# First round's mix in four banks, with its gates and routing placed between the first adapter's folding and the others'

## The reference, cut to what matters

```python
W = weights[condition]                     # 16 small 64x64 matrices
y = einsum('bct,bcd->bdt', x, W)           # "mix"
result = y @ W_base.T + b_base
probs = softmax(y @ W_gate.T); top 2 of 8 experts, renormalised -> route_w
h = einsum('bnd,erd->bner', y, A) * route_w
x = x + result + einsum('bner,eor->bno', h, B)
# second layer
y = einsum('bsi,boi->bso', x, weight[adapter_ids])     # adapter_ids are 3 to 7
scores = 8 * softmax(y @ Wr.T + br)
x = x + 2 * einsum('bshr,hor,bsh->bso', y @ A.T, B, scores)
```

## Time and profile before

| | |
|---|---|
| median of three runs | 749.4 us (748.09 to 749.75) |
| profiled execution | 748.57 us, span 746.9 us |
| busy, share of the span | PE 724.3 us (97%), DVE 335.3 (45%), ACT 114.1 (15%), POOL 57.8 (8%) |
| granted clock of PE, mean | 0.992 of 2.4 GHz |
| chain that ended last | PE 81%, issue 8%, DVE 4%, DMA 4% |

### The profile page before, as it was taken

How to read it: one execution, slowest core, us unless ns; L and a number is a source line. 1 busy time by engine, 2 the same in 40 slices (tenths; PEclk the granted TensorE clock), 3 DMA queues, 4 the chain that set the end, 5 groups by cost and what they waited for, 6 DMA issues and landing times.

```text
span 746.9 us, 12572 instructions
## 1 busy us (share of the span) xinstructions
PE 724.3 (97%) x4502; PEld 647.4 (87%) x4502; DVE 335.3 (45%) x887; ACT 114.1 (15%) x309; POOL 57.8 (8%) x115
## 2 busy tenths in 40 slices
PE   7999899999999999999999999998999999999996
PEld 7999887898888888888889888787889888998996
DVE  2000196136534644354535563464427552574644
ACT  1222300111111111111111111111111211120111
POOL 1222300001100010001000110000000100010100
PEclk9999999999999999999999999999999999999998
DMA  7999993037721883159504871277415951476552
GB/s 262 340 417 365 392 403 119 1 117 294 250 80 63 295 315 125 56 181 394 195 29 176 314 286 48 86 259 279 173 57 183 405 179 57 168 301 236 208 192 72
DMA packets 38709, 156.31 MB, mean 209 GB/s; under 512 B 8836, under 2 KB 11908, under 8 KB 28420
## 3 DMA queue, kind: packets, MB, share of 16 engines
q1 hardware_dynamic: 27714, 78.72, 28.4%
q0 software_dynamic: 9216, 71.31, 25.9%
q10 hardware_dynamic: 1730, 5.58, 1.9%
HBM read 133.24 MB, written 22.35 MB: 208 GB/s over the span
## 4 chain that ended last, share of the span: by engine, by line
PE 81%; issue 8%; DVE 4%; DMA 4%; POOL 2%; ACT 0%; POOLq 0%; ACTq 0%; DVEq 0%
PE base_ps L333 16%; PE base_ps L334 16%; PE base_ps L335 16%; PE mix_both L353 7%; DMA adapter<-folded 4%; PE low_ps L401 4%; PE out_ps L401 4%; PE mix_both L366 3%; PE base_ps L342 2%; POOL adapter L943 2%; PE out_ps L333 2%; PE out_ps L334 2%; PE out_ps L335 2%; DVE w_lo L683 1%; PE low_ps L366 1%
## 5 line engine op out<-in xcount | busy, mean ns | idle before, releaser
L333 PE MATMUL base_ps<-yT,w_hi 128*128 128x512 f32 (+1 forms) x576 | 214.7, 373 | 1.3 <-DVE xT L803 1.1
L335 PE MATMUL base_ps<-yT,w_hi 128*128 128x512 f32 (+1 forms) x576 | 211.5, 367 | 0.0
L334 PE MATMUL base_ps<-yT,w_lo 128*128 128x512 f32 (+1 forms) x576 | 211.3, 367 | 0.0
L687 DVE TENSOR_TENSOR yT<-mix_both,yT 128x512 fp32r<-128x512 f32 x64 | 44.2, 691 | 240.9 <-ACT yT L560 240.9
L333 PEld LDWEIGHTS base_ps<-yT,w_hi 128*128 128x128 f32 x576 | 108.5, 188 | 20.8 <-DVE xT L803 4.0
L335 PEld LDWEIGHTS base_ps<-yT,w_hi 128*128 128x128 f32 x576 | 108.4, 188 | 18.1
L334 PEld LDWEIGHTS base_ps<-yT,w_lo 128*128 128x128 f32 x576 | 108.6, 189 | 15.4
L342 PE MATMUL base_ps<-ag_raw,stage 128*128 128x136 f32 x640 | 76.0, 283 | 2.2 <-issue 2.2
L342 PEld LDWEIGHTS base_ps<-ag_raw,stage 128*128 128x128 f32 x640 | 75.9, 193 | 2.4 <-issue 2.4
L957 POOL DMA_DIRECT2D adapter<-folded x60 | 31.9, 532 | 576.5 <-PE low_ps L401 503.8
L699 DVE TENSOR_TENSOR x1T<-xT,x1T 128x256 fp32r<-128x256 f32 x120 | 45.3, 420 | 65.1 <-ACT x1T L567 65.1
(11 more groups left out here) (150 smaller groups left out, 747.3 us busy)
## 6 DMA issues: line engine op xcount, KB each, us to landing
adapter<-folded POOLq DMA_DIRECT2D x63, 1088.0 KB, 7.1
stage<-in_w SPq DMA_DIRECT2D x40, 512.0 KB, 8.0
x_rows<-in_x SPq DMA_DIRECT2D x32, 512.0 KB, 6.0
xT<-in_x_turned SPq DMA_DIRECT2D x16, 1024.0 KB, 7.5
out<-xT SPq DMA_DIRECT2D x28, 512.0 KB, 2.7
folded<-adapter ACTq DMA_DIRECT2D x10, 544.0 KB, 6.7
w_raw<-in_w SPq DMA_DIRECT2D x8, 256.0 KB, 8.0
w_raw<-in_w SPq DMA_DIRECT2D x4, 512.0 KB, 12.1
```

Of the source, the lines that this page charges most:

```text
L333: pe.matmul(dst, st_hi, mv_lo, start=start, stop=False, skip_group_check=True)
L334: pe.matmul(dst, st_lo, mv_hi, start=False, stop=False, skip_group_check=True)
L335: return pe.matmul(dst, st_hi, mv_hi, start=False, stop=stop, skip_group_check=True)
L687: dve.tensor_tensor(yT[:, 1, k, :], mix_ps[k % 2][:, :], yT[:, 0, k, :], ALU.subtract).then_inc(yT_lo_done, 1)
```

## The change

- SP loads `x_rows` and `g_raw` of round 0 before the second adapter's units instead of after the last adapter's.
- PE does mix and gates of round 0 after the first adapter's fold, before the loop over the others. ACT, DVE and POOL get their part of that work (both halves of mix, the copies of the gates, the routing with its Exp, and the split of `g_raw`) at the same place in their lists.
- The mix of round 0 goes through four banks instead of two (`mix_bank`); gates wait for each block as they come to it.
- The second copy of a folded unit goes to `lg` instead of `hg`, since `hg` now holds the gates' result during the other folds.

The core of the diff:

```diff
+        def mix_bank(q, r, k):
+            return hg_banks[k % 4] if isinstance(q, int) and r == 0 else mix_ps[k % 2]
...
             load_wc(0, 0)
             total = adapters_in_use(sp)
+            load_x(0, 0)
+            sp.dma_start(g_raw[:, :, 1, :], g0).then_inc(g_landed, 16)
             with sp.Fori(1, total) as n:
...
-            load_x(0, 0)
-            sp.dma_start(g_raw[:, :, 1, :], g0).then_inc(g_landed, 16)
             for k in range(KC):
                 load_w(k, 0)
...
-                if k >= 2:
-                    pe.wait_ge(yT_lo_done, at(q, r, KC, k - 1))
+                banks = 4 if isinstance(q, int) and r == 0 else 2
+                if k >= banks:
+                    pe.wait_ge(yT_lo_done, at(q, r, KC, k - banks + 1))
...
-                        if t == 0 and k in (0, KC - 1):
+                        if t == 0 and isinstance(q, int) and r == 0:
+                            if k == 0 or k >= 5:
+                                pe.wait_ge(yT_lo_done, max(5, k + 1))
+                        elif t == 0 and k in (0, KC - 1):
                             pe.wait_ge(yT_lo_done, at(q, r, KC, KC - 1 if k == 0 else KC))
+                        if t and k == 0 and isinstance(q, int) and r == 0:
+                            pe.wait_ge(yT_lo_done, 5 + t)
...
             fold(0)
+            for k in range(KC):
+                mix(0, 0, k)
+            pe.wait_ge(g_split, 1)
+            gates(0, 0)
             total = adapters_in_use(pe)
             with pe.Fori(1, total) as n:
                 fold(n)
             pe.wait_ge(unit_copied, KC * total + BANKS)
-            for k in range(KC):
-                mix(0, 0, k)
             iteration(0, 0, l1=False)
...
             take_adapter(0, e, False)
+            for k in range(KC):
+                yT_high(0, 0, k)
+            route_exp(0, 0)
             total = adapters_in_use(act)
...
             for k in range(KC):
                 yT_low(0, 0, k)
+            for t in range(TILES):
+                copy_hg(0, 0, t)
+            routing(0, 0)
             for k in range(KC):
                 split(w_hi[:, k, 0:T], w_lo[:, k, 0:T], w_raw[:, k, 0:T], w_landed[k], k)
```

More of the change, by code:

```diff
@@ L349, in mix @@
                     pe.wait_ge(wc_landed, at(q, r, 16 * PER, 16 * PER))
-                if k >= 2:
-                    pe.wait_ge(yT_lo_done, at(q, r, KC, k - 1))
+                banks = 4 if isinstance(q, int) and r == 0 else 2
+                if k >= banks:
+                    pe.wait_ge(yT_lo_done, at(q, r, KC, k - banks + 1))
                 for t in range(TILES):
-                    mm = pe.matmul(mix_ps[k % 2][:, t * P:(t + 1) * P], x_rows[:, t, k * P:(k + 1) * P], wc[:, t, :],
+                    mm = pe.matmul(mix_bank(q, r, k)[:, t * P:(t + 1) * P], x_rows[:, t, k * P:(k + 1) * P], wc[:, t, :],
                                    start=True, stop=True, skip_group_check=True)
@@ L451, in iteration @@
                 first = isinstance(q, int) and r == 0
-                if first:
-                    pe.wait_ge(g_split, 1)
-                gates(q, r)
+                if not first:
+                    gates(q, r)
                 for k in range(KC):
@@ L546, in take_unit @@
                 act.copy(adapter[:, 0, c, 0, :], base_ps[c % BANKS][:, 0:HG])
-                act.copy(hg[:, c % 4, :], base_ps[c % BANKS][:, 0:HG]).then_inc(unit_copied, 1)
+                act.copy(lg[:, c % 4, :], base_ps[c % BANKS][:, 0:HG]).then_inc(unit_copied, 1)
             def take_adapter(n, e, again):
@@ L559, in yT_high @@
                 act.wait_ge(yT_done, at(q, r, KC, k + 1))
-                act.copy(yT[:, 0, k, :], mix_ps[k % 2][:, :]).then_inc(yT_hi_done, 1)
+                act.copy(yT[:, 0, k, :], mix_bank(q, r, k)[:, :]).then_inc(yT_hi_done, 1)
             def x1T_high(q, r, i):
@@ L580, in lwT_high, with route_exp @@
                 act.copy(lwT[:, 0, toks], low_ps[:, toks]).then_inc(lwT_hi_done, 1)
+            def route_exp(q, r):
+                act.wait_ge(route_step, at(q, r, ROUTE_STEPS, 6))
+                act.activation(top_exp[:, :, :], top_d[:, :, :], ACT.Exp).then_inc(top_exp_done, 1)
             def iteration(q, r, l1=True, ahead=True):
@@ L585, in iteration @@
                     x1T_high(q, r - 1, 1)
-                act.wait_ge(route_step, at(q, r, ROUTE_STEPS, 6))
-                act.activation(top_exp[:, :, :], top_d[:, :, :], ACT.Exp).then_inc(top_exp_done, 1)
-                if l1:
+                    route_exp(q, r)
                     for i in range(2, PER):
@@ L609, in _ @@
                 take_adapter(n, e, True)
-            for k in range(KC):
-                yT_high(0, 0, k)
             iteration(0, 0, l1=False)
@@ L686, in yT_low @@
                 dve.wait_ge(yT_hi_done, at(q, r, KC, k + 1))
-                dve.tensor_tensor(yT[:, 1, k, :], mix_ps[k % 2][:, :], yT[:, 0, k, :], ALU.subtract
+                dve.tensor_tensor(yT[:, 1, k, :], mix_bank(q, r, k)[:, :], yT[:, 0, k, :], ALU.subtract
                                   ).then_inc(yT_lo_done, 1)
@@ L844, in iteration @@
             def iteration(q, r, l1=True, ahead=True, toks=ALL):
-                copy_hg(q, r, 0)
                 if l1:
+                    copy_hg(q, r, 0)
                     x1T_low(q, r - 1, 0)
-                copy_hg(q, r, 1)
-                if l1:
+                    copy_hg(q, r, 1)
                     x1T_low(q, r - 1, 1)
[L851 to L854, removed]
+                    copy_hg(q, r, 2)
+                    copy_hg(q, r, 3)
+                    routing(q, r)
                     for i in range(2, PER):
@@ L942, in low_of_adapter @@
                     pool.wait_ge(unit_copied, KC * n + c + 1 + BANKS)
-                    pool.tensor_tensor(adapter[:, 0, c, 1, :], hg[:, c % 4, :], adapter[:, 0, c, 0, :], ALU.subtract
+                    pool.tensor_tensor(adapter[:, 0, c, 1, :], lg[:, c % 4, :], adapter[:, 0, c, 0, :], ALU.subtract
                                        ).then_inc(folded_lo, 1)
             low_of_adapter(0)
+            pool.wait_ge(g_landed, 16)
+            pool.tensor_copy(g_hl[:, :, 0, :], g_raw[:, :, 1, :]).then_inc(g_split_hi, 1)
+            pool.wait_ge(g_split_hi, 1)
+            pool.tensor_tensor(g_hl[:, :, 1, :], g_raw[:, :, 1, :], g_hl[:, :, 0, :], ALU.subtract).then_inc(g_split, 1)
             total = adapters_in_use(pool)
@@ L966, in iteration @@
                         load_adapter(q, r, i)
[L969 to L972, removed]
             for p in range(2):
```

## The result

The changed kernel takes 753.52 us (median of 10 runs, 751.08 to 757.49) against 748.32 for the kernel before (10 runs, 746.48 to 752.07): ratio 1.0071, interval 1.005 to 1.0092. It is 5.2 us slower; I had forecast slower by 2.1. The profiled execution is one of its longer ones, 756.89 us with a span of 755.2, 8.3 more than that of before.

A forecast was written before the change was run, and what follows sets the result against it. PE, busy 97% of the span, bounds the kernel, so only waits and clock count. Minus 2.6, minus 1.3, plus 3.1, plus 1.7, plus 1.2 give plus 2.1 us: 750.7 from 748.57, forecast 751.0, range 746.5 to 753.6.

The forecast's parts named there:

- Direction: Whole kernel: slower by 2.1 us; chance of slower 0.47, same 0.35, faster 0.18.
- Base's start: PE in round 0, after the last fold: base begins at 105.45 us, 2.2 later than before.
- the wait for x_rows: PE, first fold to round 0's mix: x_rows lands at 28.4, PE is done at 25.3; plus 3.1 us.
- Mix in four banks, minus 2.6: Round 0's mix on PE: no waits between block pairs, 7.84 us instead of 10.44; minus 2.6.
- Routing, minus 1.3: PE ahead of the transposes at 121.09: the wait for routing's last step on DVE goes; minus 1.3 us.
- The clock, plus 1.7: Behind PE's wait for x_rows: 3.4 us at half speed, plus 1.7 us (0 to 1.9).
- The loads that now come later, plus 1.2: Ahead of base's second half, round 0: xT lands at 131.0, PE wants the bank at 130.7; plus 1.2 us.
- the store's landing: Last folded-adapter store, issued at 106.1: lands 4.5 us later, between 3.0 alone and 7.0 behind the crowded queue.
- the rest of the chain: SP's loads behind the last store: 20.2 us from round 1's first x issue to the landing of xT.
- `xT` *is really late: Rival, round 0's second half: store takes 7.0 us, PE waits 3.7; 753.2 to 754.0, clock plus 1.7 more; chance 0.14.
- The rule of the Trainium skill: Last store: DMA engines serve queues in turn, so half rate, some 4.7 us, wait 1.4; the sum didn't need it.

The follow-up runs named there:

- the two runs that isolate it: Four-bank mix alone put on the kernel before: 745.89 us, ratio 0.9972; and two-bank mix put back in the best kernel: 748.58 us, ratio 0.9994.
- with the transposes: Changed kernel plus unread transposes, 14 ahead of round 0's mix and 16 ahead of base's second half: 751.16 us, ratio 1.0034 to the kernel before.
- the best kernel: Changed kernel with round 0's wc issued by POOL, x_rows early on SP, and round 1's loads ahead of the stores' wait: 745.82 us, ratio 0.9967.
- `xT` first: Changed kernel with SP loading round 0's xT ahead of round 1's x_rows and wc: 751.99 us, ratio 1.0066 to the kernel before.
- routing late: The best kernel with round 0's gate copies and routing back behind DVE's splits, and its Exp behind ACT's folds: 746.71 us, ratio 0.997.

## Why the prediction was right and wrong

- **Direction: right. Base's start, 105.39 against 105.45: luck.** Terms of opposite sign cancelled: the first fold ended 2.1 us sooner than I took it to, for a reason that has no place in my sum; so the wait for x_rows was 4.43 and not 3.1, though x_rows landed 0.8 earlier; the clock cost 1.4 more than I had, and mix took 0.6 less. With `wc` on POOL this first wait and its clock are worth 4.7 us by the ratios, where I had 3.1 + 1.7 = 4.8. That fit is luck in part: in the traces base begins 6.4 us earlier there (99.01), and the 4.7 is uncertain by some 2.
- **Mix in four banks, minus 2.6: right in kind, undersized in the trace.** 3.2 us by the timelines of mix (10.4 to 7.2: a block takes 0.90 us, where I had 0.93, and nothing is left uncovered ahead of the gates, where I had 0.4), 2.0 to 2.1 in the medians of the two runs that isolate it, of which the second also waits for `xT`.
- **Routing, minus 1.3: not shown in the time.** The wait is gone from the trace and comes back with the edit, 1.97 us long and with a fall of the clock behind it, but its price in the median is not resolved.
- **The clock, plus 1.7: undersized.** In the profiled execution 3.1 us behind the first wait, since the low clock lasted 6.8 us and not the 3.4 that I took from the kernel before. That it falls is not sure either: with the transposes PE still stood idle for 3.65 us and stayed at 2.4 GHz.
- **The loads that now come later, plus 1.2: this step failed.** The mechanism was the right one, down to the issue of the last store at 106.1, but the wait was 4.21 us. Two terms made the difference of 3.0: the store's landing (6.6 against 4.5; the row of before said 7.0, and I took a milder value because I counted 1.2 MB of W_base still to move, when SP's queue moved 1.74 MB in that time, and b1, issued at 99.1, landed at 113.3) and the rest of the chain (21.2 against 20.2). PE wanted the bank at 130.7, as in my sum. And the clock fell behind that wait, another 2.3 us, which my sum did not hold; it stood in the rival with 7.0 us for the store. Taking this wait away wins 4.1 us of the median, against the 1.2 of my sum. The rival `xT` *is really late* is what happened in the trace: a wait of 4.21 us where it had 3.7, and the clock down once more. That its 753.2 to 754.0 hold the measured 753.5 is luck in part, for they are without that fall; with the 1.7 that the rival gives for it they would be 754.9 to 755.7.
- The rule of the Trainium skill, page "DMA: Bandwidth & Descriptors", section "Queues, rings and completion order", by which I estimated some 4.7 us for the store whatever stood on SP's queue, is not borne out as I applied it: 6.6 with loads of W_base and b1 still on it and 2.7 with nothing on it. That the engines take turns is neither shown nor refuted by that; half the rate for the store is refuted as its price.

In the medians: plus 4.7 and plus 4.1 for the two waits with their clock, and minus 2.5 for what is left when both are gone (the best kernel against before), give plus 6.3 for a measured 5.2. The 5.2 and the 2.5 are uncertain by some 1.5 us, the 4.7 and the 4.1 by some 2, so the agreement is a weak one.

## What to carry to other kernels

When work is moved ahead of the bulk of a program, the first question is what it reads and when the queue gives it; the second is what was waiting behind the old place, because everything between now ends later, and a transfer with 10 us of cover before can be the next wait. Where a new chain of issues hangs on the landing of a store, take that landing from the row under load. Moving one load forward in a full queue only passes the wait to the next load; what helped was to issue the small loads from another engine, and to take the wait away from loads that did not need it. And try the simplest part of a change by itself first: here four banks alone, which moves no transfer, won as much as the whole change did after both of its new waits had been mended.

## What the runs showed of the hardware that I had not expected

- An issue on SP is not always cheap: with 13 loads of some 512 KB issued ahead of it, part of them still to land, one `wc` issue of usually 0.48 us took 6.4.
- The granted clock stayed at 1.00 over an idle of 3.65 us (24.9 to 28.5 us, with transposes ahead of it), and over one of 2.95 with none ahead of it (`xT` first), and fell in the kernel before after one of 1.85 ahead of 321.5 us and with routing late after 1.97. The length of one idle does not tell alone, and a fall lasted 3.4 us in some places and 6.8 in others.
- The spread of the best kernel's runs, 740.65 to 747.72 us, goes in part with the clock: 1.000 in its profiled 743.06 and 0.991 in its slowest, but 1.000 also in one of 746.67.
